# A fused transformer block on one core: when rows are normalised, their statistics taken and low halves split around the last layer's openings

## The reference, cut to what matters

```python
x = x + L0_xattn(_layernorm(x), ctx, ...)     # self-attention on the context
x = x + L0_ffn(_layernorm(x), ...)            # mixture of experts and a shared expert
x = x + L1_xattn(_layernorm(x), ctx, ...)     # 16 query heads, 8 key/value heads of 128
x = x + L1_ffn(_layernorm(x), ...)            # below

# L1_ffn: fwht is a normalised Walsh-Hadamard transform over the last dimension
x = fwht(x * SU_ug) / SCALE                   # over 512
x_up, x_gate = x @ W_up.T * ..., x @ W_gate.T * ...     # 512 -> 2048
x = silu(x_gate) * x_up
x = fwht(x * SU_dp) / SCALE                   # over 2048 (folded into the down weights before)
x = x @ W_down.T * ...                        # 2048 -> 512
```

## Time and profile before

| | |
|---|---|
| time, median of 3 runs | 2226.91 us (2225.63 to 2227.18) |
| profiled execution: span | 2227.4 us |
| profiled execution: its own time | 2229.22 us |
| TensorE matmuls (PE) busy | 2181.6 us, 98% of the span |
| VectorE (DVE) busy | 1569.3 us, 70% |
| ScalarE (ACT) busy | 1109.8 us, 50% |
| GpSimd (POOL) busy | 554.2 us, 25% |
| mean granted TensorE clock | 0.995 of full |
| attention's last matmul, last layer's first after the barrier | 1700.73 and 1701.78 us |

### The profile page before, as it was taken

The page is one execution under the profiler, slowest core; times in us unless marked ns, Lnnn a source line. Parts: engine busy times, 40 slices in busy tenths (PEclk is TensorE's granted clock), DMA queues, the critical chain, the costliest instruction groups (busy, mean ns, idle before and its releaser), DMA issues. The chain is left out here.

```text
span 2227.4 us, 32324 instructions
## 1 busy us (share of the span) xinstructions
PE 2181.6 (98%) x10903; PEld 1819.0 (82%) x10903; DVE 1569.3 (70%) x3163; ACT 1109.8 (50%) x1969; POOL 554.2 (25%) x551
## 2 busy tenths in 40 slices
PE   8999999999999999999999999999998999999999
PEld 6778788888999977888888888888876788778887
DVE  7864375546777766777777777777776888688787
ACT  5532220114556566666666666666665443444343
POOL 4432545521111171001000001000034225322111
PEclk9999999999999999999999999999999999999999
DMA  6431321125787784101110100101101212223221
GB/s 229 133 108 48 94 62 34 29 73 211 259 282 277 243 315 164 38 21 38 47 28 28 28 28 28 38 19 38 29 11 57 71 53 80 67 72 95 81 71 62
DMA packets 88284, 205.42 MB, mean 92 GB/s; under 512 B 9136, under 2 KB 30128, under 8 KB 85360
## 3 DMA queue, kind: packets, MB, share of 16 engines
q1 hardware_dynamic: 79936, 177.00, 23.5%
q0 software_dynamic: 8240, 27.01, 4.8%
HBM read 160.20 MB, written 43.78 MB: 92 GB/s over the span
## 5 line engine op out<-in xcount | busy, mean ns | idle before, releaser
L2251 ACT ACTIVATE route_weights<-route_weights,xa_minus_max 128x512 f32<-128x512 f32 x256 | 184.9, 722 | 187.8 <-DVE xa_minus_max L2412 187.7
L2428 DVE TENSOR_TENSOR xa_late_hi<-xa_ps_t,route_wv_hi 128x512 fp32r<-128x512 f32 x256 | 174.8, 683 | 120.2 <-ACT route_wv_hi L2260 120.1
L2187 POOL TENSOR_TENSOR route_kv_lo<-route_rows,route_kv_hi 128x1024 fp32r<-128x1024 f32 x32 | 77.0, 2407 | 695.4 <-ACT route_kv_hi L2225 695.4
L2260 ACT ACTIVATE route_wv_hi<-xa_ps_t 128x512 fp32r<-128x512 f32 x256 | 151.5, 592 | 95.9 <-PE xa_ps_t L2624 67.5
L2412 DVE CUSTOM_DVE_ANT_0 route_weights<-xa_ps_s,route_mask_bias 128x512 f32<-128x512 f32 x256 | 175.6, 686 | 0.6 <-issue 0.6
L2624 PEld LDWEIGHTS xa_ps_t<-ident,route_weights 128*128 128x128 f32 x1024 | 126.5, 139 | 36.5 <-issue 3.9
L2624 PE MATMUL xa_ps_t<-ident,route_weights 128*128 128x128 f32 x1024 | 153.3, 272 | 1.9 <-DVE xa_late_hi L2428 1.9
L94 PE MATMUL xa_ps_p<-route_wv_hi,route_kv_hi 128*128 128x512 f32 x288 | 119.1, 414 | 3.4 <-DVE xa_late_hi L2428 1.7
L1098 ACT ACTIVATE moe_silu<-moe_ps_gate 128x512 f32<-128x512 f32 x44 | 26.3, 597 | 190.1 <-PE moe_ps_gate L96 190.1
L94 PE MATMUL xa_ps_p<-late_xT_hi,late_wq_hi 128*128 128x512 f32 (+1 forms) x264 | 114.1, 432 | 1.0 <-DVE late_wq_lo L2906 1.0
L96 PE MATMUL xa_ps_p<-route_wv_hi,route_kv_lo 128*128 128x512 f32 x288 | 113.1, 393 | 0.0
(11 more groups left out here) (689 smaller groups left out, 6814.6 us busy)
## 6 DMA issues: line engine op xcount, KB each, us to landing
route_weights<-in_ffn_w SPq DMA_DIRECT2D x37, 512.0 KB, 3.6
route_weights<-in_expert_w SPq DMA_DIRECT2D x12, 1408.0 KB, 7.2
route_weights<-wd_folded SPq DMA_DIRECT2D x64, 256.0 KB, 2.6
ex_w_raw<-in_expert_w SPq DMA_DIRECT2D x10, 1408.0 KB, 6.5
moe_y<-ex_y SPq DMA_DIRECT2D x39, 256.0 KB, 3.8
route_weights<-in_expert_w SPq DMA_DIRECT2D x12, 768.0 KB, 9.2
ex_w_raw<-in_expert_w SPq DMA_DIRECT2D x11, 768.0 KB, 8.8
route_weights<-in_xa_w SPq DMA_DIRECT2D x16, 512.0 KB, 3.6
```

The source lines that it names most:

```text
L2187: pool.tensor_tensor(kvl[b % 2][:], rawkv[b % 2], f32(kvh[b % 2][:]), ALU.subtract).then_inc(M.kv_ready, 1)
L2251: act.activation(prob[slot][:], prob[slot][:], ACT.Exp, bias=nmx[:, slot:slot + 1], scale=-1.0, accum_out=tot[:, slot:slot + 1]).then_inc( ...
L2260: act.activation(PTh[:, :, tt * P:(tt + 1) * P], psT[tt % 2][:].rearrange("p (k n) -> p k n", k=TT), ACT.Copy).then_inc(M.pt_hi, 1)
L2428: dve.tensor_tensor(PTl[:, :, tt * P:(tt + 1) * P], psT[tt % 2][:].rearrange("p (k n) -> p k n", k=TT), f32(PTh[:, :, tt * P:(tt + 1) * P] ...
```

## The change

It has these parts. In the attention, GpSimd flies all rows of batch 1 (4 to 7) instead of row 4 alone; for that rows 6 and 7 have places of their own, GpSimd also signs them, and ScalarE normalises rows 4 to 7 there, rows 4 and 5 at earlier places. The statistics of rows 0 to 7 are taken at the places of `STAT_PLACES`, one or two at a time. In the last layer, the normalises of plain steps stand between the copies of turned and of rotated rows; the normalises of rows 10 and 11 are one step earlier than their flies, which keep their steps; `add_y` of batch 0 moves from step 16 to step 17, behind the low halves of the turned rows; and in steps 3, 4 and 20 the splits and input sums stand in another order.

```diff
@@ -2216,7 +2216,8 @@
                 for t in range(1, TT):
                     row_fly(pool, L, t)
                 next_rstd(1)
-                row_fly(pool, L, TT)
+                for t in range(TT, 2 * TT):
+                    row_fly(pool, L, t)
             @block.scalar
             def _(act):
@@ -2333,16 +2334,19 @@
                                 u_high(act, L, 2, psP[0])
                             if at == (7, -1):
                                 u_high(act, L, 3, psO[0])
+                                row_norm(act, G, L, TT)
+                                split_gate_up_hi(act, G, L, 0)
                             if at == (7, 1):
-                                split_gate_up_hi(act, G, L, 0)
+                                row_norm(act, G, L, TT + 1)
                             if at == (7, 2):
                                 rot_copy(act, L, 1, 0, psS[0])
                                 rot_high(act, L, 1, 0, psS[0])
                             if at == (7, 3):
                                 rot_copy(act, L, 1, 1, psS[1])
                                 rot_high(act, L, 1, 1, psS[1])
-                                row_norm(act, G, L, TT)
-                                row_norm(act, G, L, TT + 1)
+                                act.wait_ge(M.kv_ready, GROUPS * B)
+                                row_norm(act, G, L, TT + 2)
+                                row_norm(act, G, L, TT + 3)
                                 split_gate_up_hi(act, G, L, 1)
                         beside((ul, -1))
@@ -2489,26 +2493,20 @@
                             if which != "last":
                                 return
-                            if at == (3, 3):
-                                dve.wait_ge(M.x_added, (pair - 1) * TT + TT)
-                                for t in range(TT):
+                            if at in STAT_PLACES:
+                                for t in STAT_PLACES[at]:
+                                    dve.wait_ge(M.x_added, (g * B + t // TT) * TT + t % TT + 1)
                                     next_stats(t)
                             if at == (5, 1):
                                 u_low(dve, L, 0, psO[1])
                             if at == (5, 3):
                                 u_low(dve, L, 1, psO[0])
                             if at == (6, 1):
-                                dve.wait_ge(M.x_added, (pair - 1) * TT)
-                                next_stats(TT)
-                                next_stats(TT + 1)
                                 rot_low(dve, L, 0, 0, psO[1])
                             if at == (6, 2):
                                 rot_low(dve, L, 0, 1, psP[1])
                             if at == (6, 3):
                                 u_low(dve, L, 2, psP[0])
-                                next_stats(TT + 2)
-                            if at == (7, 0):
-                                next_stats(TT + 3)
                             if at == (7, -1):
                                 u_low(dve, L, 3, psO[0])
                             if at == (7, 1):
@@ -2523,6 +2521,7 @@
                             split_o(g, 0)
                         beside((ul, -1))
                         normalise(i + 2, 2, halves(g, ul, 2))
+                        beside((ul, "scaled"))
                         turned_low(i, 0)
                         if has_pv:
                             proj_low(last_pv(pair, h, left < 2), o_hi[out_buf(b, 1 - h)], o_lo[out_buf(b, 1 - h)])
@@ -2542,6 +2541,7 @@
                             masked_max(i + 5, 1, nb)
                             normalise(i + 4, 0, halves(g, ul, 4))
                         turned_low(i + 2, 2)
+                        beside((ul, "turned"))
                         if has_output:
                             add_x(pair - 1, ob, 3 if h else 0)
                         beside((ul, 2))
@@ -2550,6 +2550,7 @@
                             masked_max(i + 6, 2, nb)
                             invert(i + 5, 1).then_inc(M.inv_ready, 1)
                         turned_low(i + 3, 3)
+                        beside((ul, "last turned"))
                         if left >= 2:
                             proj_low(next_q(pair, h), qh[h], ql[h])
                         if has_output and h == 0:
@@ -2561,6 +2562,8 @@
                         beside((ul, 3))
                 next_stats, _, _ = ln_vector(dve, L.R, x, None, None)
+                STAT_PLACES = {(2, "last turned"): (0,), (3, "scaled"): (1,), (3, "turned"): (2,), (3, "last turned"): (3,),
+                               (5, "scaled"): (4, 5), (5, "last turned"): (6,), (6, "scaled"): (7,)}
                 groups(dve, body)
                 proj_low(FINAL_PV, o_hi[out_buf(B - 1, 1)], o_lo[out_buf(B - 1, 1)])
                 split_gate_up_lo(dve, G, L, 1)
@@ -2830,6 +2833,7 @@
 EVENTS = final_events(STEPS)
 NSTEPS, NEVENTS = len(STEPS), len(EVENTS)
 LAST_PLAIN = max(s for s, st in enumerate(STEPS) if st.kind == "plain")
+FIRST_B = LAST_PLAIN - PLAIN + 1
 TAILS = [r for st in STEPS for r in st.tail]
@@ -2863,7 +2867,7 @@
     L.R = ln_stat_buffers(sb, sem)
     L.gu_hi = [L.wqh, G.kvh[0]]
     L.gu_lo = [L.wql, G.kvl[0]]
-    L.places = {}
+    L.places = {6: G.rows[:, 0:S], 7: G.rows[:, S:2 * S]}
     L.normed = sem("normed")
     L.signed = sem("signed")
     L.flown = sem("flown")
@@ -2915,7 +2919,7 @@
 FLY = 4
-VECTOR_ROWS = (6, 7, 12, 13, 14, 15)
+VECTOR_ROWS = (12, 13, 14, 15)
 def row_place(L, t):
@@ -3061,7 +3065,7 @@
         kept = [G.rows[:, i * S:(i + 1) * S] for i in range(KEPT - KEPT // 2)]
         kept += [G.wv_room[:, i * S:(i + 1) * S] for i in range(KEPT // 2)]
         part.append(G.wv_room[:, KEPT // 2 * S:(KEPT // 2 + 1) * S])
-        L.places = {10: kept[4], 11: kept[5], 12: part[2], 13: L.row[0], 14: L.row[1], 15: kept[4]}
+        L.places |= {10: kept[4], 11: kept[5], 12: part[2], 13: L.row[0], 14: L.row[1], 15: kept[4]}
         thi = [room[:, 0:S] for room in (G.first_lo, G.mask_room)]
         tlo = [room[:, S:2 * S] for room in (G.first_lo, G.mask_room)]
         psG = [ps(f"ps_gate{i}") for i in range(2)]
@@ -3102,7 +3106,8 @@
         M.t_even = sem("t3_t4")
         TURNS = {0: (4, 5), 1: (6, 7), 15: (8, 9), 16: (10, 11), 17: (12, 13), 18: (14, 15)}
         ROTATES = {0: 2, 1: 3, 15: 4, 16: 5, 17: 6, 18: 7}
-        NORMS = {1: (6, 7), 11: (8, 9), 13: (10,), 14: (11,), 16: (12, 13, 14), 17: (15,)}
+        NORMS = {11: (8, 9), 12: (10,), 13: (11,), 16: (12, 13, 14), 17: (15,)}
+        FLIES = {11: (8, 9), 13: (10,), 14: (11,), 16: (12, 13, 14), 17: (15,)}
         STATS = {6: (8,), 7: (9,), 8: (10,), 9: (11,), 11: (12, 13, 14, 15)}
         RSTD = {10: 2, 12: 3}
         X_ORDER = ("b1", "b2", "t1", "t2", "t3", "t4"), ("a1", "a2", "t1", "b2", "t2", "t3", "t4")
@@ -3187,7 +3192,6 @@
                     pool.wait_ge(M.t_odd, 2 * p + 2)
                     pool.tensor_tensor(X.raw_t4, X.raw_a[1], X.raw_t2, ALU.subtract).then_inc(M.t_even, 1)
-                row_fly(pool, L, TT + 1)
                 for s in range(NSTEPS):
                     if is_pair(s + 1):
                         weight_sums(s + 1)
@@ -3197,7 +3201,7 @@
                         t4(STEPS[s + 1].pair)
                     if s in RSTD:
                         rstd(RSTD[s])
-                    for t in NORMS.get(s, ()):
+                    for t in FLIES.get(s, ()):
                         row_fly(pool, L, t)
             @block.scalar
@@ -3243,12 +3247,26 @@
                             act.wait_ge(M.down_done, STEPS[TAILS[n - 2]].read + 1)
                         act.activation(thi[n % 2], kept[n % KEPT], ACT.Copy).then_inc(M.tail_hi, 1)
-                def beside(s):
+                def turned(s):
                     for i, t in enumerate(TURNS.get(s, ())):
                         u_high(act, L, t, bank_of(s, i))
+
+                def rotated_rows(s):
                     if s in ROTATES:
                         for half in range(2):
                             rot_copy(act, L, ROTATES[s], half, bank_of(s, half))
+
+                def norms(s):
+                    for t in NORMS.get(s, ()):
+                        if t == 10:
+                            act.wait_ge(M.tail_ready, 5)
+                        if t == 11:
+                            act.wait_ge(M.tail_ready, 6)
+                        if t == 12:
+                            act.wait_ge(M.kept_ready, STEPS[s].pairs)
+                        if t >= 13:
+                            act.wait_ge(L.turned, {13: 9, 14: 10, 15: 11}[t])
+                        row_norm(act, G, L, t)
                 def silu(s, n, src):
                     j = STEPS[s].j
@@ -3282,11 +3300,14 @@
                         if s == PLAIN - 2:
                             x_high(0, "b1")
                             x_high(0, "b2")
+                        plain_silu(s)
                         if s == LAST_PLAIN:
+                            split_down(st.event)
```

(47 more changed lines are left out.)

## The result

The change made the kernel faster, by less than forecast, and just outside the stated range: 2209.76 us (median of 4 runs, 2209.53 to 2211.28) against 2227.05 us before (4 runs beside them, 2225.63 to 2229.29), ratio 0.9923 with a 95% interval of 0.9906 to 0.994. The forecast was 2201.0 us with a range of 2196.5 to 2209.5. The profiled execution's span went from 2227.4 to 2207.8 us, 19.6 less, where 25.9 was forecast.

The account below looks back on a forecast made before the run. TensorE, busy 98% of the span, was taken as the bound. Seven terms summed to 25.9 us, taking the span from 2227.4 to 2201.5 us; corrected by 2.3 us to the median, the forecast was 2201.0 us, range 2196.5 to 2209.5.

Parts of the forecast that it names:

- term B: End of attention: earlier copies and statistics against GpSimd flying rows 4 to 7 there; -1.3 us, bounds -2.6 and +0.5.
- A: Attention, four statistics in a row on VectorE: spread into its idle places, TensorE's excess goes; -3.7 us, bounds -3.9 and -1.5.
- C: Last layer, step 1: rows 6 and 7 flown before the barrier, TensorE's waits for them go; -7.4 us, bounds -7.5 and -5.0.
- D: Opening of the first pairs: down-weight split and x_low moved behind split_sums; -3.6 us, bounds -4.0 and -1.2.
- E: Before batch 1's first plain step: row 10's earlier fly brings GpSimd's weight sums forward; -0.5 us, bounds -0.6 and 0.
- F: Step 16, wait for late_xT_lo: earlier normalises and add_y behind the turned halves remove it; -7.5 us, bounds -7.7 and -4.5.
- G: Last plain step, wait for ffn_down_lo: split ahead of the hidden product, x_low behind; -1.9 us, bounds -3.8 and -0.2.
- Rivals: 2: One of two big waits returns in VectorE's queue (step 17) or ScalarE's (step 2): 2207 to 2211 us; chance 0.10.
- Rival 1: GpSimd as new lock-holder halves several gains, barrier waits 1 us for row 7: gain 19.6 us, 2207.3 us; chance 0.17.

Follow-up runs that it names:

- openings_only: Kernel before with only the last layer's part of the change; attention as before, rows 6 and 7 still flown in step 1: 2208.43 us, ratio 0.9907.
- rows67_stat5: Changed kernel with rows 6 and 7 signed and flown behind the barrier and row 5's statistics one place later: 2202.13 us, ratio 0.9894.
- tiny_gpsimd: Changed kernel with rows 6 and 7 flown behind the barrier, plus one GpSimd 128x16 addition waiting for TensorE's last attention matmul: 2206.84 us, ratio 0.991.
- extra5: Changed kernel with rows 6 and 7 flown behind the barrier, plus five unused GpSimd 128x512 additions at the attention's end: 2204.09 us, ratio 0.9902.
- attention_only: Kernel before with only the attention's part of the change (statistics, normalises and flies of rows 4 to 7): 2223.17 us, ratio 0.9972.
- extra2: Changed kernel plus two unused GpSimd 128x512 additions behind row 7's fly, before the barrier: 2210.38 us, ratio 0.9923.

## Why the prediction was wrong

The failed step is in **term B**: "GpSimd is then only 0.6 us ahead of the block's end", with 1698.9 for the end of four flies against 1699.5, and as the bound that GpSimd is late by 2 us at a cost of 0.5 over before. Two things in it were wrong, and the second was not in the range at all.

- *When the flies end.* A's 3.9 us bring both engines forward, and I left them out of both ends; with them the forecast is 1695.6 for TensorE and 1695.0 for GpSimd. Measured: 1696.38 and 1697.52. Of GpSimd's 2.5 us, 0.8 are the first fly's start (1677.99 for 1677.2), 1.4 two operations that stood beside VectorE's low halves of weights and took 1.86 and 1.60 us in place of 1.30 and 0.73, and the rest is mostly row 5's wait for its normalise (0.66, where 0.5 was planned). Being 1.1 us late would alone have cost about 1.1, an estimate by which the engines go on 0.3 us after GpSimd as they do after TensorE.
- *What it means to be there.* The barrier opened 3.13 us after GpSimd's last instruction. The rows of before did not show such a thing: at this barrier GpSimd was done 6.1 us before the others went on (1695.27 to 1701.42). At the end of the first block it was done 2.96 us before, at 132.44, where TensorE had ended 0.3 us ahead. A margin is in both, and neither tells how little would have been enough. I took "nothing shown" for "nothing there" and set the bound from below at GpSimd's last instruction.

With the half clock behind it, B and the barrier came to -0.55 + 6.4 = +5.85 us in place of -1.3: 7.2 us off, more than the whole miss of 6.3 us in the span. The other 2.5 of the 8.8 us between forecast and median (2201.0 and 2209.76) are, all but 0.2, the correction by 2.3 us that I took from the profiled execution of before, which lay above its median; that of the changed kernel (2209.61) lay on it.

The terms, with TensorE's times in the two traces:

| | forecast | measured | from |
|---|---|---|---|
| A statistics | -3.7 | -3.9 | 7.53 to 3.66 us between the same instructions |
| B tail of the attention | -1.3 | -0.55 | last matmul 4.74 earlier, less A and 0.3 by which the transposes at A already start earlier |
| barrier | 0 (B's upper bound holds 2 us of it) | +6.4 | above |
| C rows 6 and 7 | -7.4 | -7.3 | 1704.59 to 1728.41 against 1706.24 to 1722.74 |
| D and E openings | -4.1 | -3.3 | what is left between 1728.41 and 1921.34 against 1722.74 and 1912.38 |
| F step 16 | -7.5 | -7.7 | 1921.34 to 1932.54 against 1912.38 to 1915.85 |
| G last plain step | -1.9 | -2.9 | what is left up to the end |

Without the barrier the seven terms give 25.65 us against 25.9 forecast. **A** is the full excess, but 1.6 us of it (7.53 less 5.96) is a half clock that openings_only does not have behind the same two waits, so that much hangs on the one trace that was read. And the cover was not what I took it for: a new wait of 0.9 us stands in unit 5. Of the 1.90 us of idle time there in the earlier trace rows 1.6 had come from that half clock, since in openings_only they are 0.33; in rows67_stat5 one statistic (0.81 us) fills the place and the low half follows without a pause. **C** went as said, but the reason given was only one of two: openings_only shows that the order on ScalarE alone gives 6.1 of the 7.3 us; the flies in the attention were needed only for the rest, a wait of 1.03 us. **D** kept 0.32 us, as "split_sums ends within 0.5 us of its need" said. It also has a new wait of 1.01 us at 1755.42 for an x_low of the first pair, which the prediction does not name; VectorE works without a pause from 1744.69 until that x_low is done. **F** held in all its steps: VectorE waited 0.49 us for ScalarE's copy, the low halves were ready at 1911.77, 0.83 us before TensorE asked (0.8 was forecast), and add_y (2.48 us) delays nobody. **G** kept 0.38 and 0.77 us, both behind VectorE's low halves held by GpSimd.

Of the holding the trace has three clear cases: 2.78 us beside a GpSimd operation of 2.59, 2.89 and 2.67 in step 20, for subtractions that take 0.68 elsewhere. Each began while the GpSimd operation ran and ended 0.54 to 0.55 us after it (1744.76 after 1744.22, 1947.39 after 1946.84, 1957.22 after 1956.67). So the subtraction's end is set by GpSimd's; that it lasts "as long as the latter", as the prediction read it, comes of when it began. This is the rule of the Trainium skill ("SBUF — State Buffer", section "SBUF: two separate sides"), by which VectorE and GpSimd hold a shared port pair for a whole instruction and the other is blocked; these traces agree. By it alone the sum would have been about 2 us less; D, E and G together came out 0.2 us better than forecast, so it did not decide the sum.

Rivals: 2 (a big wait comes back, 2207 to 2211) gave the right time by luck, since it named VectorE's and ScalarE's queues and not the barrier. Rival 1 named the barrier's wait for row 7 but priced it at 1 us. The prediction's own mark of failure, "the barrier is reached by GpSimd over 1 us late", is what happened. What stays open is what GpSimd does in the 3.1 to 3.5 us, and why tiny_gpsimd and extra5 show 3.4 to 3.5 where three others show 3.13. Nor is it the same at every barrier. At the end of the first block, which no edit touches, attention_only has

```profile
132.46 0.24 POOL L1025 IOTA moe_counts<- 128x128 int32 x1 [2.70 <-POOLq L439]
```

and the engines went on 0.3 us after TensorE, as everywhere; an arrival 3.13 us after GpSimd's last instruction would have held them. Whether the last instruction, the place of the barrier in the program or something else makes the difference, no run here separates.

## What to carry to other kernels

Plan GpSimd's arrival at a barrier as its last instruction's end plus some 3.5 us, until the trace of your barrier shows that less is enough (2.70 us was at another one here), and leave work behind the barrier that does not fit in front of it. When one edit both reorders a queue and moves work out of it, try the reordering alone: here it gave 6.1 of the 7.3 us for rows 6 and 7, and the moving cost 6.4 us elsewhere. A wait's price includes the matmuls at half clock behind it, but that part comes and goes between versions, so it is no firm gain. And idle time of an engine before an edit may be the effect of a stall in front of it (1.90 us in unit 5 with the half clock, 0.33 without), so it is not room for other work.

## What the runs showed of the hardware

- At the attention's end the engines leave the barrier 3.13 us after GpSimd's last instruction (the change, attention_only, extra2), 3.45 and 3.51 in tiny_gpsimd and extra5, against 0.3 us after VectorE's or TensorE's. At the first block's end GpSimd was done only 2.70 us before (attention_only) and did not hold it. The 3.13 us are no latency of GpSimd's semaphores within a block: in openings_only TensorE starts on row 7 at 1720.18, 0.06 us after GpSimd's last butterfly (1719.40 + 0.72).
- The half clock behind the wait at the barrier lasted 12 matmuls (the change, after 4.61 us), 8 (extra2, after 6.82; attention_only, after 4.61) and 7 (tiny_gpsimd, after 4.12), and none followed 1.86 us in extra5. Two waits of 0.67 and 1.18 us were followed by 8 before and by none in openings_only, and none followed the wait of 3.58 us before, in step 20 (the rows below). Neither whether it comes nor its length is set by that of the wait alone, so it is a source of 1 to 2 us of spread between versions. The Trainium skill, "TensorE: Matmul & The Clock Gate", section "What's actually happening", says that the number of slow matmuls at a kernel's start differs from run to run of the same kernel. The traces here, one execution each of different kernels, show a like spread in the middle of a kernel.

```profile
1965.03 0.47 PE L94 MATMUL ffn_ps_y<-ffn_down_hi,ffn_hidden_hi 128*128 128x512 f32 x1 [3.58 <-DVE ffn_down_lo L3364]
1965.34 0.39 PE L95 MATMUL ffn_ps_y<-ffn_down_lo,ffn_hidden_hi 128*128 128x512 f32 x1
```
